# Sending seven attention units of ten, not five, through a DMA transpose, and adding the two output parts on DVE

## The chip, the cores and the metric

One core of one Trainium2 chip runs the kernel. The metric is the device time in microseconds (us) of one execution of the whole program. Names of engines: PE is the matmul engine, DVE the vector engine, ACT the scalar (activation) engine, POOL the GpSimd engine, SP the queue from which most DMAs are issued.

## The reference, cut to what matters

A cross attention with 8 batches, 512 queries, 20 heads of 16 columns, 508 text tokens and 4 image tokens of width 512:

```python
q   = heads(x @ W_q);  k_t = heads(text @ W_k);  v_t = heads(text @ W_v)
probs_t  = softmax(q k_t^T / 4)                       # [8, 20, 512, 508]
text_out = probs_t v_t
qsem = l2norm(probs_t @ text);  sem = qsem @ l2norm(ip)^T
probs_ip = softmax(q k_ip^T / 4 + 0.5 * sem) * spatial_mask
out = (text_out + probs_ip v_ip) @ W_out + b_out + x
```

The norm of `probs_t @ text` is taken without forming it: with the Gram matrix G = text text^T, the squared norm of a query row p is p G p^T.

## The kernel before, in words

**Three stages.** First, for each batch, the projections, G (`u_parts`) and the values (`v_parts`) are made and stored to HBM (until about 345 us). Then comes the main loop, with which the change deals (about 349 to 1686 us). Last, the l2 norms, the image tokens and the output projection (until the end).

**The main loop's unit.** A unit is one head of one batch with 128 query rows: 8 x 20 x 4 = 640 units, in 16 rounds of `ROUND` = 40. In each round the 40 units are written out, and `Fori` loops repeat a round; PE's loops differ from those of the other engines. Each engine has its own hand-written order, and the engines meet in semaphores. For unit j:

- PE, `scores` (L1394): 128x508 scores into one of two banks (`S_BANK`). It waits until `exp` of unit j-2 has read that bank. PE issues it eight units ahead (`LEAD`).
- DVE, `row_maximum` (L1090), then ACT, `exp` (L807), into `probs`, a ring of ten.
- The probabilities are needed turned (tokens on partitions), as the sum of two fp16 parts. There are two ways:
  - **odd j, "turned by DMA"**: ACT copies the high part into `flat` (`flat_hi`, L816), POOL makes the remainder (L579), and SP issues one DMA transpose of both parts (`turn`, L438) into `turned`, a ring of `RING` = 4. For these units ACT adds a constant to the exponent's bias first (`shift`, L796). POOL then adds the remainder onto `probs` as the weight of the norm (`weigh_odd`, L586).
  - **even j, "plain"**: PE turns the fp32 probabilities (`transposes`, L1403, four a unit, three units ahead), ACT takes the high part (`hi`, L832), DVE the remainder (`lo`, L1105); ACT also writes half of the high part of the unturned rows (`halve`, L823), and POOL subtracts it from `probs` (`weigh_even`, L593).
- PE, `unit` (L1428 to L1434): for the high part, four times one matmul with the values into `o` (L1428) and two with G into `y` (L1429, L1430); for the remainder four matmuls with the values (L1434). It waits for the turned data and for the norm of unit j-2 (two `y` banks).
- DVE, `norm` (L1099): `y` times `probs`, summed along the row. DVE's order in step j is `row_maximum(j)`, `norm(j-9)`, and in even steps `lo(j-6)`.
- ACT, `drain_out` (L838): once in two units, the output bank into `out_raw`. POOL, `reduce_head` (L600 a copy of 4 columns, L601 an addition of 128x80), once in four units: the two parts of the output are added into `reduced`.

**Queues.** SP issues the transposes in order, and once in 20 units, after unit 9, ten loads: nine for the next five heads' q and k (`load_group`, L362 and L366) and one for their values (L369). A turn waits for POOL's remainder and for `unit_done` of the unit that last used the slot of the ring.

Of the kernel before, what the change touches and what calls it, by code (L numbers as in the profile page):

```python
# [5 lines left out]
def xattn_kernel(  # L6
# [46 lines left out]
    P = 128  # L53
# [27 lines left out]
    PAIRS_PER_ROUND = ROUND // 2  # L81
# [7 lines left out]
    with stack:  # L89
# [174 lines left out]
        odd_weight_ready = sem("odd_weight_ready")  # L264
        even_weight_ready = sem("even_weight_ready")
# [75 lines left out]

        def nth(rnd, j):

            rnd, j = at(rnd, j)
            return PAIRS_PER_ROUND * rnd + j // 2

        def landed(eng, rnd, j):

            rnd, j = at(rnd, j)
            r = j // 2 % RING  # L350
            need(eng, turned_landed[r], 16 * (PAIRS_PER_ROUND // RING * rnd + j // 2 // RING + 1))

        def flat_rows(j):
            return flat[:, j // 2 % RING]
# [18 lines left out]
        def _(sp):  # L373
# [57 lines left out]
            def turn(rnd, j):  # L431
# [3 lines left out]
                need(sp, unit_done, ROUND * rnd + j + 1 - 2 * RING)  # L435
                apart(sp)
                r = j // 2 % RING
# [57 lines left out]
        def _(pool):  # L495
# [86 lines left out]
            def weigh_odd(rnd, j):  # L582
# [3 lines left out]
                nc.gpsimd.tensor_tensor(own, own, flat_rows(at(rnd, j)[1])[:, 1, :, 0:TP], ALU.add).then_inc(odd_weight_ready, 1)  # L586

            def weigh_even(rnd, j):
# [4 lines left out]
                nc.gpsimd.tensor_tensor(own, own, half_hi[:, at(rnd, j)[1] // 2 % RING, :], ALU.subtract).then_inc(even_weight_ready, 1)  # L593

            def reduce_head(g, slot):

                pool.wait_ge(out_drained, 2 * g + 2)
                apart(pool)
                raw = out_raw[:, 2 * slot:2 * slot + 2].rearrange("p a u c -> p (a u) c")
                nc.gpsimd.tensor_copy(reduced[:, g, :, VW_PART:RCOLS], raw[:, :, VCOLS - 1:VCOLS])  # L600
                nc.gpsimd.tensor_tensor(reduced[:, g, :, 0:VW_PART], raw[:, :, 0:VW_PART],  # L601
                                        raw[:, :, VW_PART:2 * VW_PART], ALU.add).then_inc(head_reduced, 1)

            REDUCE_AT = LEAD + 1 + ST - 1
# [16 lines left out]
            for j in (-6, -4, -2):  # L621
                weigh_even(ROUNDS, j)
# [911 lines left out]
```

## Time and profile before

| what | value |
|---|---|
| median of 3 runs | 1804.03 us (1801.88 to 1806.68) |
| the profiled execution's own time | 1804.91 us |
| its span | 1803.2 us |
| busy: PE / DVE / ACT / POOL | 96% / 69% / 66% / 68% of the span |
| granted clock of PE in the main loop | 0.99 to 1.00 of full speed |

Busy shares are means over the three stages. In the rows below, the third column of a timeline is the engine; `[0.94 <-DVE ...]` behind a row is the idle time of that engine before it and what ended it. Instructions of an engine overlap a little, so the distance between two starts is what an instruction costs its engine, and it is some 0.05 to 0.1 us less than its duration.

### The profile page before, as it was taken

The numbers are of one execution on the slowest core, as the hardware profiler recorded it, in microseconds if no ns is written. First come the engines' busy times: TensorE is split into PE (matmuls) and PEld (weight loads), VectorE is DVE, ScalarE is ACT, GpSimd is POOL, SyncE is SP. The second block draws the span as 40 slices with busy tenths as digits, with TensorE's granted clock in tenths as the row PEclk, the third lists the DMA queues.
The fourth block names the chain that finished last, engine by engine and source line by source line (L and its number), as shares of the span: only waits on it lengthen the run. The fifth ranks groups of instructions, "written<-read, shape, count | busy, mean of one in ns | idle before, by whom it ended". The sixth has DMA issues, their size and how long they took to land.

```text
span 1803.2 us, 48758 instructions
## 1 busy us (share of the span) xinstructions
PE 1736.2 (96%) x14421; PEld 1103.9 (61%) x14421; DVE 1244.6 (69%) x2872; ACT 1182.8 (66%) x2644; POOL 1230.7 (68%) x1414
## 2 busy tenths in 40 slices
PE   4999999599999999999999999999999999999899
PEld 2767666466666666665666666656566666666455
DVE  5445554277777777777777777767677777777684
ACT  2455455477777777777777777777777777777321
POOL 2122212388888888888788888878888888888310
PEclk7999999799999999999999999999999999999999
DMA  5445554734566445445555555465555445553133
GB/s 161 113 139 142 137 144 123 171 68 92 101 103 119 92 91 111 92 91 92 105 92 100 99 121 92 91 106 92 90 90 113 93 91 103 104 96 66 37 103 101
DMA packets 429986, 187.83 MB, mean 104 GB/s; under 512 B 387128, under 2 KB 417472, under 8 KB 429792
## 3 DMA queue, kind: packets, MB, share of 16 engines
q1 hardware_dynamic: 427488, 183.41, 49.4%
q10 hardware_dynamic: 2304, 2.14, 0.4%
q8 instruction: 84, 1.38, 0.3%
q14 instruction: 110, 0.90, 0.2%
HBM read 67.21 MB, written 34.39 MB: 56 GB/s over the span
## 4 chain that ended last, share of the span: by engine, by line
POOL 37%; PE 35%; issue 22%; DVE 3%; POOLq 1%; ACT 1%; DMA 0%; SPq 0%; ACTq 0%; DVEq 0%
POOL probs L586 16%; POOL probs L593 16%; PE bank L1286 13%; PE bank L1429 6%; PE bank L1430 4%; PE bank L1494 3%; POOL reduced L601 2%; POOL wkv L579 2%; PE bank L1344 2%; PE bank L1394 2%; PE bank L1403 1%; PE bank L1495 1%; POOL reduced L600 1%; PE bank L1434 1%; DVE reduced L1017 1%
## 5 line engine op out<-in xcount | busy, mean ns | idle before, releaser
L1429 PE MATMUL bank<-u_sb,late 127*128 127x508 f16 x2560 | 944.0, 375 | 0.0
L1430 PE MATMUL bank<-u_sb,late 127*128 127x508 f16 (+3 forms) x2560 | 761.1, 297 | 0.0
L1090 DVE TENSOR_REDUCE neg_max<-bank 128x1 f32<-128x508 f32 x640 | 439.3, 687 | 342.0 <-PE bank L1394 341.7
L579 POOL TENSOR_TENSOR wkv<-probs,wkv 128x508 f16<-128x508 f32 x320 | 358.8, 1121 | 199.6 <-ACT wkv L816 199.6
L1428 PE MATMUL bank<-v_ring,late 127*128 127x41 f16 x2560 | 468.1, 183 | 4.4 <-DVE late L1105 4.4
L1099 DVE SCALAR_TENSOR_TENSOR probs<-bank,probs 128x508 f32<-128x508 f32 x640 | 432.9, 677 | 4.6 <-PE bank L1430 4.6
L1428 PEld LDWEIGHTS bank<-v_ring,late 127*128 127x128 f16 x2560 | 246.7, 96 | 233.4 <-DVE late L1105 4.5
L593 POOL TENSOR_TENSOR probs<-probs,late 128x508 f32<-128x508 f32 x320 | 368.6, 1152 | 0.0
L586 POOL TENSOR_TENSOR probs<-probs,wkv 128x508 f32<-128x508 f32 x320 | 357.6, 1118 | 0.0
L1429 PEld LDWEIGHTS bank<-u_sb,late 127*128 127x128 f16 x2560 | 247.8, 97 | 166.2 <-issue 1.1
L1394 PE MATMUL bank<-x_sb,work 96*128 96x508 bf16 x640 | 241.8, 378 | 28.2 <-DMA x_sb<-k_parts 12.2
L1430 PEld LDWEIGHTS bank<-u_sb,late 127*128 127x128 f16 x2560 | 244.8, 96 | 0.0
L807 ACT ACTIVATE probs<-bank,neg_max 128x508 f32<-128x508 f32 x320 | 216.8, 677 | 38.7 <-DVE neg_max L1090 20.8
L796 ACT ACTIVATE exp_bias<-neg_max 128x1 f32<-128x1 f32 x320 | 64.7, 202 | 257.1 <-DVE neg_max L1090 257.1
L1105 DVE SCALAR_TENSOR_TENSOR late<-bank,late 127x512 f16<-127x512 f32 x320 | 219.5, 686 | 7.5 <-ACT late L832 7.5
L816 ACT ACTIVATE wkv<-probs 128x508 f16<-128x508 f32 x320 | 201.4, 629 | 25.1 <-ACT probs L807 17.4
L807 ACT ACTIVATE probs<-bank,exp_bias 128x508 f32<-128x508 f32 x320 | 216.2, 676 | 0.0
L1403 PEld LDWEIGHTS bank<-ident,probs 128*127 128x127 f32 x1280 | 190.9, 189 | 9.2
L823 ACT ACTIVATE late<-probs 128x508 f16<-128x508 f32 x320 | 195.8, 612 | 0.7
L1403 PE MATMUL bank<-ident,probs 128*127 128x128 f32 x1280 | 195.1, 275 | 0.0
L546 POOL TENSOR_TENSOR late<-work,late 128x512 bf16<-128x512 f32 (+3 forms) x48 | 55.2, 1151 | 202.9 <-ACT late L723 202.9
L832 ACT ACTIVATE late<-bank 127x512 f16<-127x512 f32 x320 | 184.9, 578 | 0.0
(166 smaller groups left out, 1803.7 us busy)
## 6 DMA issues: line engine op xcount, KB each, us to landing
x_sb<-k_parts SPq DMA_DIRECT2D x192, 79.4 KB, 3.5
x_sb<-in_x SPq DMA_DIRECT2D x16, 640.0 KB, 5.0
reduced<-in_ctx SPq DMA_DIRECT2D x32, 256.0 KB, 5.1
work<-q_parts SPq DMA_DIRECT2D x32, 240.0 KB, 3.4
u_parts<-u_sb SPq DMA_DIRECT2D x8, 825.5 KB, 4.2
u_sb<-u_parts SPq DMA_DIRECT2D x8, 825.5 KB, 5.4
v_parts<-v_sb SPq DMA_DIRECT2D x8, 820.0 KB, 8.0
v_ring<-v_parts SPq DMA_DIRECT2D x32, 205.0 KB, 3.7
```

The costliest lines, as they stand in the source:

```text
L579: nc.gpsimd.tensor_tensor(rows[:, 1, :, 0:TP], probs[:, j % PROB_RING, :].rearrange("p (k t) -> p k t", k=TT), rows[:, 0, :, 0:TP], ALU.su ...
L586: nc.gpsimd.tensor_tensor(own, own, flat_rows(at(rnd, j)[1])[:, 1, :, 0:TP], ALU.add).then_inc(odd_weight_ready, 1)
L593: nc.gpsimd.tensor_tensor(own, own, half_hi[:, at(rnd, j)[1] // 2 % RING, :], ALU.subtract).then_inc(even_weight_ready, 1)
L807: nc.scalar.activation(probs[:, j % PROB_RING, :], bank[S_BANK + j % 2][:, 0:T], ACT.Exp, bias=bias[:, j % 4:j % 4 + 1]).then_inc(probs_re ...
L1090: nc.vector.tensor_reduce(neg_max[:, j % 4:j % 4 + 1], bank[S_BANK + j % 2][:, 0:T], AX.X, ALU.max, negate=True)\
L1099: nc.vector.scalar_tensor_tensor(own, bank[Y_BANK + j % 2][:, 0:T], 1.0 if j % 2 == 1 else 2.0 * PROB_SCALE, own, ALU.mult, ALU.mult, accu ...
L1286: last = nc.tensor.matmul(out, stationary(a), moving(m), start=(n == 1), stop=(n == len(SPLIT) * len(terms)))
L1394: nc.tensor.matmul(bank[S_BANK + j % 2][:, 0:T], q_ring[:, n, h, st * P:(st + 1) * P], k_ring[:, n, h, :], start=True, stop=True).then_inc ...
L1403: last = nc.tensor.transpose(bank[PT_BANK + j // 2 % 2][0:TP, k * P:(k + 1) * P], probs[:, j % PROB_RING, k * TP:(k + 1) * TP], ident[:, :])
L1428: nc.tensor.matmul(o, hi_k, v_ring[0:TP, n, h, k, :], start=(k == 0), stop=False)
L1429: nc.tensor.matmul(y, hi_k, u_sb[0:TP, par, GH[k]:GH[k] + T], start=(k == 0), stop=False)
L1430: done = nc.tensor.matmul(y[:, k * TP:T], hi_k, u_sb[0:TP, par, UL[k]:UL[k] + U_COLS[k]], start=False, stop=(k == TT - 1))
```

## The change

Of each ten units, j mod 10 = 2, 5 and 9 are plain, and the seven others are turned by DMA. All ring indices and counts follow from lists (`OWN[j]` is the number of unit j among those of its kind). The rings keep their sizes, so that a slot of `turned` comes back after four turned units, which are five or six units apart, not eight. POOL's order becomes: remainder of j, weight of a turned unit two steps after it, weight of a plain unit five steps after it. `reduce_head` goes from POOL to DVE, behind `norm` and `lo` in every fourth step. `shift(j+1)` stands ahead of `flat_hi(j)` or `halve(j)` on ACT wherever j+1 is turned. ACT's loop has a last round written out, so that 14 rounds of 16 are in its `Fori` and not 15.

```diff
+    PLAIN_AT = (2, 5, 9)
+    PLAIN = [j for j in range(ROUND) if j % 10 in PLAIN_AT]
+    TURNED = [j for j in range(ROUND) if j % 10 not in PLAIN_AT]
+    OWN = {j: n for kind in (PLAIN, TURNED) for n, j in enumerate(kind)}
...
+        def done_before(rnd, j, back):
+
+            n = OWN[j] - back
+            own = kind(j)
+            return ROUND * (rnd + n // len(own)) + own[n % len(own)] + 1
...
@@ SP: turn, turns
-                need(sp, unit_done, ROUND * rnd + j + 1 - 2 * RING)
+                need(sp, unit_done, done_before(rnd, j, RING))
...
-                for j in range(1, ROUND, 2):
-                    turn(rnd, j)
+                for j in range(ROUND):
+                    if is_turned(j):
+                        turn(rnd, j)
...
@@ POOL
-            def reduce_head(g, slot):
-
-                pool.wait_ge(out_drained, 2 * g + 2)
-                apart(pool)
...
+            TURNED_AT, PLAIN_LAG = 2, 5
 
             def units(rnd, first):
                 for j in range(ROUND):
-                    if j % 2 == 1:
+                    if is_turned(j):
                         remainder(rnd, j)
-                        if not (first and j < 2):
-                            weigh_odd(rnd, j - 2)
-                    elif not (first and j < 6):
-                        weigh_even(rnd, j - 6)
-                    if j % ST == REDUCE_AT % ST and not (first and j < REDUCE_AT):
-                        reduce_head(ROUND // ST * rnd + (j - REDUCE_AT) // ST, (j - REDUCE_AT) // ST % 2)
+                    if is_turned(j - TURNED_AT) and not (first and j < TURNED_AT):
+                        weigh_turned(rnd, j - TURNED_AT)
+                    if not is_turned(j - PLAIN_LAG) and not (first and j < PLAIN_LAG):
+                        weigh_plain(rnd, j - PLAIN_LAG)
...
@@ ACT
-                if not (first and j < 2 * RING):
-                    landed(act, rnd, j - 2 * RING)
-                    need(act, odd_weight_ready, nth(rnd, j) + 1 - RING)
+                if not (first and OWN[j] < RING):
+                    landed(act, rnd, j, 1)
+                    need(act, turned_weight_ready, nth(rnd, j) + 1 - RING)
...
-                need(act, unit_done, ROUND * rnd + j - 3)
-                r = j // 2 % 2
+                need(act, unit_done, done_before(rnd, j, 2))
+                r = OWN[j] % 2
...
                 for j in range(ROUND):
-                    if j % 2 == 1 and not (first and j < HI_AT):
+                    if not is_turned(j - HI_AT) and not (first and j < HI_AT):
                         hi(rnd, j - HI_AT)
+                    if first and j == 0:
+                        shift(rnd, 0)
                     exp(rnd, j)
-                    if j % 2 == 0:
+                    if is_turned(j + 1) and not (last and j + 1 == ROUND):
                         shift(rnd, j + 1)
+                    if is_turned(j):
+                        flat_hi(rnd, j, first)
+                    else:
                         halve(rnd, j)
-                    else:
-                        flat_hi(rnd, j, first)
...
-            units(0, True)
-            with act.Fori(1, ROUNDS) as rnd:
-                units(rnd, False)
...
+            units(0, True, False)
+            with act.Fori(1, ROUNDS - 1) as rnd:
+                units(rnd, False, False)
+            units(ROUNDS - 1, False, True)
...
@@ DVE
+            def reduce_head(g, slot):
+
+                dve.wait_ge(out_drained, 2 * g + 2)
+                apart(dve)
+                raw = out_raw[:, 2 * slot:2 * slot + 2].rearrange("p a u c -> p (a u) c")
+                nc.vector.tensor_copy(reduced[:, g, :, VW_PART:RCOLS], raw[:, :, VCOLS - 1:VCOLS])
+                nc.vector.tensor_tensor(reduced[:, g, :, 0:VW_PART], raw[:, :, 0:VW_PART],
+                                        raw[:, :, VW_PART:2 * VW_PART], ALU.add).then_inc(head_reduced, 1)
+
             LO_AT = 6
+            REDUCE_AT = LEAD + 1 + ST - 1
 
             def units(rnd, first):
                 for j in range(ROUND):
                     row_maximum(rnd, j)
                     if not (first and j < LEAD + 1):
                         norm(rnd, j - LEAD - 1)
-                    if j % 2 == 0 and not (first and j < LO_AT):
+                    if not is_turned(j - LO_AT) and not (first and j < LO_AT):
                         lo(rnd, j - LO_AT)
+                    if j % ST == REDUCE_AT % ST and not (first and j < REDUCE_AT):
+                        reduce_head(ROUND // ST * rnd + (j - REDUCE_AT) // ST, (j - REDUCE_AT) // ST % 2)
...
@@ PE: unit
-                if (j + T_LEAD) % 2 == 0 and not (last and j + T_LEAD >= ROUND):
+                if not is_turned(j + T_LEAD) and not (last and j + T_LEAD >= ROUND):
                     transposes(rnd, j + T_LEAD)
...
-                if j % 2 == 1:
+                if is_turned(j):
                     landed(pe, rnd, j)
```

## Rows read from the trace of the kernel before

**Rows 1.** The page: busy time of each engine over the span.
```profile
PE 1736.2 (96%) x14421; PEld 1103.9 (61%) x14421; DVE 1244.6 (69%) x2872; ACT 1182.8 (66%) x2644; POOL 1230.7 (68%) x1414
```

**Rows 2.** Windows of the main loop: stretch, length, busy (x instructions) by engine, clock, DMA share.
```profile
core 0: us, PE busy (x) PEld busy (x) DVE busy (x) ACT busy (x) POOL busy (x), PEclk, DMA share, GB/s
600.00:800.00 200.00, 199.80 (x1860) 126.67 (x1859) 152.16 (x343) 152.34 (x343) 172.97 (x196) 1.00 0.52 99
```

**Rows 3.** Timeline, PE's scores matmuls and transposes: start, duration.
```profile
1000.99 0.37 PE L1394 MATMUL bank<-x_sb,work 96*128 96x508 bf16 x1
1002.81 0.37 PE L1394 MATMUL bank<-x_sb,work 96*128 96x508 bf16 x1
1003.02 0.60 PE L1403 MATMUL bank<-ident,probs 128*127 128x128 f32 x4
1005.07 0.38 PE L1394 MATMUL bank<-x_sb,work 96*128 96x508 bf16 x1
```

**Rows 4.** PE's idle time in the main loop (350 to 1700 us): total, times, longest.
```profile
PE bank L1394 <- issue: 8.6, 3, 3.3
PE bank L1394 <- ACT probs L807: 6.8, 9, 2.4
```

**Rows 5.** Timeline, POOL, of the same stretch.
```profile
1007.53 1.12 POOL L586 TENSOR_TENSOR probs<-probs,wkv 128x508 f32<-128x508 f32 x1
1008.60 1.15 POOL L593 TENSOR_TENSOR probs<-probs,late 128x508 f32<-128x508 f32 x1
1009.69 0.19 POOL L600 COPY reduced<-out_raw 128x4 f32 x1
1009.84 0.36 POOL L601 TENSOR_TENSOR reduced<-out_raw 128x80 f32 x1
```

**Rows 6.** Timeline, DVE: one even step whole, and the next step's start.
```profile
1001.40 0.69 DVE L1090 TENSOR_REDUCE neg_max<-bank 128x1 f32<-128x508 f32 x1 [0.97 <-PE bank L1394]
1002.00 0.68 DVE L1099 SCALAR_TENSOR_TENSOR probs<-bank,probs 128x508 f32<-128x508 f32 x1
1002.61 0.69 DVE L1105 SCALAR_TENSOR_TENSOR late<-bank,late 127x512 f16<-127x512 f32 x1
1003.22 0.69 DVE L1090 TENSOR_REDUCE neg_max<-bank 128x1 f32<-128x508 f32 x1
```

**Rows 7.** Timeline, ACT, to the end of one loop iteration and the first exp of the next.
```profile
1004.57 0.58 ACT L832 ACTIVATE late<-bank 127x512 f16<-127x512 f32 x1
1005.04 0.68 ACT L807 ACTIVATE probs<-bank,exp_bias 128x508 f32<-128x508 f32 x1
...
1006.28 0.22 ACT L838 ACTIVATE out_raw<-bank 128x82 f32<-128x82 f32 x1
1008.59 0.69 ACT L807 ACTIVATE probs<-bank,neg_max 128x508 f32<-128x508 f32 x1 [2.09 <-DVE neg_max L1090]
```

**Rows 8.** DVE additions and a tensor_scalar of 128x80 after the main loop: ns min/median/max.
```profile
L1165 DVE TENSOR_TENSOR probs<-late,probs x8: 1832/1850/1952, 1690.0 to 1769.2; 128x80 f32<-128x80 f32 x8
L1166 DVE TENSOR_TENSOR probs<-probs x8: 241/242/243, 1691.9 to 1771.1; 128x80 f32<-128x80 f32 x8
L1163 DVE TENSOR_SCALAR probs<-late x8: 193/195/195, 1689.1 to 1768.2; 128x80 f32<-128x80 f32 x4, 128x80 f32 x4
```

**Rows 9.** Timeline after the main loop, POOL and DVE at the same time.
```profile
1689.33 2.42 POOL L638 TENSOR_TENSOR late<-reduced,late 128x1280 f32<-128x1280 f32 x1 [2.60 <-DVE late L1158]
1689.99 1.85 DVE L1165 TENSOR_TENSOR probs<-late,probs 128x80 f32<-128x80 f32 x1
```

**Rows 10.** The transposes' issue on SP (ns min/median/max), and their time to landing.
```profile
L438 SPq DMA_TRANSPOSE late<-wkv x320: 1231/1233/3463, 355.7 to 1669.7; - x160
...
DMA to landing us min/median/max: 3.0/3.0/5.7
```

**Rows 11.** Timeline, SP, around one group's loads.
```profile
1061.19 9.25 SPq L438 DMA_TRANSPOSE late<-wkv  x3
1070.78 1.27 SPq L362 DMA_DIRECT2D work<-q_parts  x3
1077.13 2.83 SPq L438 DMA_TRANSPOSE late<-wkv  x2
```

More of the change, by code:

```diff
@@ L619, in _ @@
                 units(rnd, False)
-            weigh_odd(ROUNDS, -1)
-            for j in (-6, -4, -2):
-                weigh_even(ROUNDS, j)
-            for g in range(HEADS - 1 - (REDUCE_AT - ST) // ST, HEADS):
-                reduce_head(g, g % 2)
+            for j in range(PLAIN_LAG):
+                if j < TURNED_AT and is_turned(j - TURNED_AT):
+                    weigh_turned(ROUNDS, j - TURNED_AT)
+                if not is_turned(j - PLAIN_LAG):
+                    weigh_plain(ROUNDS, j - PLAIN_LAG)
             pool.wait_ge(head_reduced, HEADS)
@@ L821, in halve @@
                 act.wait_ge(probs_ready, ROUND * rnd + j + 1)
[L822 to L823 removed]
+                need(act, plain_weight_ready, nth(rnd, j) + 1 - RING)
+                nc.scalar.activation(half_hi[:, slot_of(j), :], probs[:, j % PROB_RING, :], ACT.Copy, scale=0.5)\
                   .then_inc(half_ready, 1)
@@ L857, in units @@
                         drain_out(ROUND // ST * rnd + g, st // 2, g % 2)
-            units(0, True)
-            with act.Fori(1, ROUNDS) as rnd:
-                units(rnd, False)
-            for u in range(UNITS - DRAIN_AT, UNITS):
-                if u % 2 == 0 and u >= UNITS - HI_AT + 1:
-                    hi(ROUNDS, u - UNITS)
+            units(0, True, False)
+            with act.Fori(1, ROUNDS - 1) as rnd:
+                units(rnd, False, False)
+            units(ROUNDS - 1, False, True)
+            for j in range(DRAIN_AT):
+                if j < HI_AT and not is_turned(j - HI_AT):
+                    hi(ROUNDS, j - HI_AT)
+                u = UNITS + j - DRAIN_AT
                 if u % 2 == 1:
@@ L1122, in _ @@
                 norm(ROUNDS, j - LEAD - 1)
-                if j % 2 == 0 and j < LO_AT:
+                if j < LO_AT and not is_turned(j - LO_AT):
                     lo(ROUNDS, j - LO_AT)
+            for g in range(HEADS - 1 - (REDUCE_AT - ST) // ST, HEADS):
+                reduce_head(g, g % 2)
             dve.wait_ge(head_reduced, HEADS)
@@ L1416, in unit @@
                     pe.wait_ge(values_loaded[n], 16 * (rnd + 1))
-                if j % 2 == 1:
+                if is_turned(j):
                     landed(pe, rnd, j)
-                    both = [turned[0:TP, j // 2 % RING, a] for a in range(2)]
+                    both = [turned[0:TP, slot_of(j), a] for a in range(2)]
                 else:
                     pe.wait_ge(lo_ready, nth(rnd, j) + 1)
-                    both = [a[:, j // 2 % 2, :].rearrange("p (k s) -> p k s", k=TT) for a in (probs_hi, probs_lo)]
+                    both = [a[:, OWN[j] % 2, :].rearrange("p (k s) -> p k s", k=TT) for a in (probs_hi, probs_lo)]
                 need(pe, norms_done, ROUND * rnd + j - 1)
@@ L1444, in _ @@
                 t = j - LEAD + T_LEAD
-                if t >= 0 and t % 2 == 0:
+                if t >= 0 and not is_turned(t):
                     transposes(0, t)
```

50 lines of the change are left out of this document (24 added, 26 removed).

## The prediction

> **What bounds the kernel now.** I read the busy shares first, then the windows, then the timeline. Over the span PE is at 96% and no other engine above 69% [rows 1]. In the main loop the windows say it more sharply: PE 100% busy at full clock, POOL 86%, DVE and ACT 76%, the DMA engines 52% [rows 2]. A busy PE need not be PE at its peak, so the timeline has to show that it doesn't wait: from one scores matmul to the next it takes 1.82 us in a unit without transposes (1000.99 to 1002.81) and 2.26 us in one with them (1002.81 to 1005.07) [rows 3]. So a pair costs 4.08 us, and 320 pairs 1306 us. PE's idle time there that an engine or its own issue caused is only 15 us [rows 4]. PE's instruction stream is the bound, and POOL is the next one.
>
> **1. The transposes that go (gain).** Of ten units three are plain, not five: 640 x 0.2 = 128 units lose their four transposes. One unit's transposes cost PE 2.26 - 1.82 = 0.44 us [rows 3]. 128 x 0.443 = **-56.7 us** (in ten units 19.52 us where it was 20.40). The bound from above is that nothing takes their place; that is what the rest is about.
>
> **2. POOL.** Between starts, a remainder or a weight takes POOL 1.07 us (1007.53 to 1008.60), a plain weight 1.09, and the reduce_head pair about 0.15 + 0.31 = 0.46 [rows 5]. Per ten units before: 10 x 1.07 + 5 x 1.09 + 2.5 x 0.46 = 17.3 of 20.4, 85%, as the window has it [rows 2]. After: 14 x 1.07 + 3 x 1.09 = 18.25 of 19.52, 93.5%. With reduce_head kept it would be 19.4, no room at all. POOL keeps up, with 1.3 us spare in ten units. I went through its order by hand: at most two jobs pile up (remainder 0, weight 8, plain weight 5 in a row), which makes remainder 1 about 1.3 us late, and that is gone by unit 3. Nobody needs a remainder that soon (see 5). Cost 0; if the cover goes, rival C.
>
> **3. ACT and DVE.** ACT per ten units by durations: it loses two hi and two halve and gets two flat_hi and two shifts, 88% full before and after; in between I find every exp done about 1 us ahead of the scores matmul that waits for it. Cost 0. What does change is the place where ACT's loop turns. Today the first exp of an iteration starts 2.09 us after the last instruction of the one before (drain 1006.28 + 0.22, exp 1008.59) [rows 7], and PE hardly feels it: PE's waits for exp are 6.8 us in nine places [rows 4]. The cover is thin: this exp starts 3.5 us after its scores (1005.07) and the scores matmul that needs it comes 4.08 us after them. After the change the iteration ends on shift(0) of the next round, which can't run before row_maximum of that unit, 1.10 us after its scores (0.41 to the start, 0.69 long) [rows 3, 6]; halve and drain follow, then the 2.1 us, then hi(35) takes 0.47 us of ACT before exp (1004.57 to 1005.04) [rows 7]. By that exp ends some 5.2 us after its scores, where PE wants it after 4.08: 1.15 us of stall at each of 13 turns, 15 us, less some 4 that it costs already: **+11 us**. Bounds: 0 (the turn stays hidden, as now) and 13 x 1.7 = 22, if DVE's own turn makes the row maximum late by 0.5 as well. The Trainium skill, "Runtime: NRT & Kernel Launch", section "Instruction fetch mechanics", says that a taken branch out of the prefetched window stalls the sequencer; by that, too, the stall is at the turn alone, and the 2.09 us agree.
>
> **4. reduce_head on DVE.** The trace has no such pair on DVE in the loop. Its cost in DVE's own time is small: an addition of 128x80 takes 0.24 us [rows 8], a tiny copy some 0.1 more. But the same rows have another addition of the same shape, L1165, that takes 1.85 us all eight times. The timeline shows why: it starts 0.66 us after a POOL instruction of 2.42 us (1689.33 to 1691.75) and ends at 1691.84, 0.09 after it [rows 9]. Both its inputs lie in SBUF, as those of reduce_head's addition do; norm and lo have one input in PSUM and run at 0.68 beside a POOL that is 86% busy [rows 2, 6]. So I take it that reduce_head's addition waits until the POOL instruction under way ends, and POOL is now under way 93% of the time. The Trainium skill ("SBUF — State Buffer", on who interferes with whom) states it as a lock: a DVE instruction with two SBUF inputs and a GpSimd instruction that reads SBUF exclude each other. The rows agree.
>
> What does it cost the path? DVE's step after a scores matmul at time 0: row_maximum at 0.41, norm at 1.01, done at 1.7 (lo, where there is one, at 1.62) [rows 3, 6]. PE must not start a unit's y matmuls before norm of two units earlier; with units of 1.82 us that norm has about 0.3 us of slack, 0.75 where the unit is 2.26 long. A reduce_head in a step delays the next row_maximum and with it the next norm. Going through the five reduce steps of 20 units with POOL's order from part 2: in step 8, which has lo ahead of it, the addition waits for remainder 7, the next step is 0.85 us late, and PE stalls 0.55; in the four others the lateness is 0 to 0.4, mostly within the slack, together 0.1. That is 0.65 us in 20 units, x 32 = **+21 us**. Lower bound 0 (no meeting, as with L1166), upper bound for this one wait: a whole POOL instruction, 1.07 less 0.3 slack, for each of 160 heads, 123 us. I take 21 because a wait has a mean of half an instruction and four of five steps can swallow that.
>
> **5. The transposes that come.** 448 in place of 320. SP's issue takes 1.23 us each [rows 10], 7 x 1.23 = 8.6 of 19.5 us: fits. The data moves in a small part of the 3.0 us to landing; the DMA share of 52% [rows 2] goes to some 70%. The slot of `turned` is now released by a unit that is five or six ahead, not eight: the turn starts at the latest four units before its own (7.3 to 7.7 us) and lands after 3.0 [rows 10]. Covered, but for unit 10 after the loads: turn 8 waits for unit 3; issue 1.23, then the ten loads, 6.7 us from the end of one turn (1061.19 + 9.25) to the start of the next (1077.13) [rows 11], then 3.0 to 5.7 to landing [rows 10]. That is 11.2 to 13.9 us after the start of unit 4, and PE wants it after 12.0. Up to 1.9 us late in each of 31 places, mostly not at all: **+3 us** (0 to 59).
>
> **Sum.** 1804.9 (the profiled execution's time; 1.7 above its span, 0.9 above the median) - 56.7 + 11 + 21 + 3 = 1783; less the 0.9 it is **1782** against the median.
>
> **The rivals.**
> A. *The lock costs nothing that counts* (DVE's addition falls into POOL's gaps). Then the sum lacks 21: 1761. For it: 24% of DVE's loop is idle [rows 2]. Against: L1165, eight of eight [rows 8].
> B. *Slower: DVE waits twice for each head.* The copy ahead of the addition is an SBUF to SBUF instruction, too. If it also waits for POOL's instruction, POOL's next one is queued by then and goes ahead of the addition, which waits a whole 1.07 us more. Its place is the step after each reduce; hardly any slack is left there, so nearly all of it reaches PE: 160 x (1.07 less about 0.1) = 155 on top of the forecast, 1937; less where POOL has gaps by then, from 1850. It decides from 0.26 us of PE stall a head on: (56.7 - 11 - 3)/160 is where the gain is used up. For it: a tensor_scalar of 128x80 between SBUF and SBUF takes 195 ns, the addition 242 [rows 8], so one-input instructions run in another, faster way. Against: no row has such a copy beside POOL. The Trainium skill, same page and section, says that a copy between SBUF and SBUF in a two-port mode excludes GpSimd wholly; by that rule this rival is what happens, if four elements are enough for the mode, which no row here shows.
> C. *POOL becomes the bound*: 18.25 us, its own turn of the loop (some 2 us in 40 units, 0.5 in ten), and what DVE's additions block, 2.5 x 0.3. That makes 19.5, level with PE; each 0.5 us of ill-timed idle in ten units is 32 us: about 1795.
> D. *Late landings after the loads*: the upper end of part 5, +56: about 1838, slower. For it: landings of 5.7 occur. Against: the median is 3.0.
>
> **How the numbers follow.** A measurement of this kernel can tell 0.3% (5.4 us) from no change. Chances: the forecast 0.45, A 0.20, B 0.18, C 0.11, D 0.06. The range goes from 1755 (A with a hidden loop turn) to 1838 (D and the dearer ends of parts 3 and 4) and leaves out B. Faster than 1798.6: most of the forecast (0.41), all of A, 0.08 of C: 0.69. Within 0.3%: 0.07. Slower: B, D: 0.24.
>
> **What would show it.** Right: PE at 1.82 and 2.26 us a unit, with 768 transposes and not 1280; POOL at 91 to 94% in the windows; DVE's 128x80 addition far over 0.24 us in the mean (0.6 to 0.8) and PE stalls behind norm, once in 20 units and at ACT's turn. Wrong: the copy of 4 columns at 0.5 us or more and the addition over 1.1 (B), POOL without gaps (C), PE idle until a DMA landing (D), or the addition at 0.24 (A). That the two kinds are not 7 to 3 can't be: the lists fix it.

## The result, and the profile after the change

The changed kernel takes 1870.03 us (median of 4 runs, 1865.09 to 1873.23), where the kernel before takes 1804.12 on the same chip: a ratio of 1.0368 [1.0339, 1.0397]. It is 66 us slower. The forecast was 1782, within 1755 to 1838, so sign and range were both wrong. The profiled execution took 1873.23, its span is 1871.5.

The page of the changed kernel: busy time of each engine, to be held against [rows 1], and from its costliest groups the copy of `reduce_head` (busy us, mean ns | idle before it, and what ended most of it):

```profile
span 1871.5 us, 48870 instructions
PE 1711.9 (91%) x13909; PEld 1045.4 (56%) x13909; DVE 1335.6 (71%) x3064; ACT 1140.2 (61%) x2644; POOL 1291.7 (69%) x1222
...
L1127 DVE COPY reduced<-out_raw 128x4 f32 (+1 forms) x160 | 119.1, 745 | 53.1 <-ACT out_raw L846 51.9
```

The windows of the main loop, same columns as [rows 2]:

```profile
core 0: us, PE busy (x) PEld busy (x) DVE busy (x) ACT busy (x) POOL busy (x), PEclk, DMA share, GB/s
600.00:800.00 200.00, 183.55 (x1640) 109.37 (x1641) 151.54 (x343) 135.27 (x319) 167.19 (x153) 0.97 0.65 112
```

PE has 512 records fewer (128 units times four transposes), as planned. But in the loop it is now busy 92% of the time and not 100%, and POOL, which was to rise to 93.5%, is at 84%: nobody is full any more. An engine that was the bound and has become idle says that a wait was added. The next view names it. PE's waits from 350 to 1760 us, that is, in the main loop (engine, line, what it waited for: us in total, times, longest):

```profile
PE bank L1456 <- DVE probs L1113: 52.3, 76, 2.4
PE bank L1422 <- ACT probs L815: 29.1, 19, 2.7
PE bank L1456 <- issue: 14.5, 17, 1.4
PE bank L1456 <- DMA late<-wkv: 9.1, 10, 1.4
```

Where [rows 4] had 6.8 and 8.6 us, there is now a unit's first matmul (L1456) waiting for norm (L1113), the scores matmul (L1422) waiting for exp (L815), and a little for landings. Idle time counts from the end of the last record; the distance between starts shows the whole of a stall. So I took, for every unit, the distance from its scores matmul to its first own matmul less the shortest that occurs (0.21 us, or 0.65 with transposes between them), and the distance from the end of the unit before to the scores matmul:

| PE's stalls in the loop, us | before | after |
|---|---|---|
| first matmul of a unit waits for norm | 3.8 (no single one over 0.2) | 91.2 (132 times, those with a late landing among them) |
| scores matmul waits for exp, at the turn of ACT's loop | 2.8 | 24.3 |
| late landing of a transpose | 0 | 10.4 |
| other, at the loop's start | 8.9 | 6.4 |
| stretches in which PE runs at 1.2 GHz (granted clock 0.50) | 3.4 long | 30.6 long |

The stalls grew by 116.8. At 1.2 GHz PE's matmuls take up to twice as long (from a scores matmul to the unit's first own 0.40 us at 779.38, where it is 0.21 at full clock). PE is busy for 27.4 of these 30.6 us, and for 3.0 of the 3.4 before; half of the difference, about 12, is what the clock costs, by estimate. With the gain: -56.7 + 116.8 + 12 = +72, and the loop, from its first unit to its last, grew by 66.6 (1324.4 to 1391.0). The sum is 5 too high; that a part of the slow stretches is counted in the stalls as well would explain it, but isn't shown.

**The wait for norm.** Of the 91.2 us, 22.5 lie in unit 33 of each round, at the loop turn. The rest sits in four units of twenty, those whose number mod 20 is 10 (23.9, the late landings included), 14 (22.2), 18 (21.6) and 2 (7.9). A `reduce_head` in step j makes norm(j-8) late, for which PE waits ahead of unit j-6: these are steps 16, 0, 4 and 8. The fifth, step 12, costs nothing. The timeline of the changed kernel shows one whole (start, duration, engine):

```profile
1005.71 0.22 ACT L846 ACTIVATE out_raw<-bank 128x82 f32<-128x82 f32 x1
1005.88 1.12 POOL L598 TENSOR_TENSOR wkv<-probs,wkv 128x508 f16<-128x508 f32 x1
1006.16 0.38 PE L1422 MATMUL bank<-x_sb,work 96*128 96x508 bf16 x1
1006.19 0.83 DVE L1127 COPY reduced<-out_raw 128x4 f32 x1 [0.60 <-ACT out_raw L846]
1006.94 0.23 DVE L1128 TENSOR_TENSOR reduced<-out_raw 128x80 f32 x1
1006.96 1.19 POOL L605 TENSOR_TENSOR probs<-probs,wkv 128x508 f32<-128x508 f32 x1
1007.09 0.67 DVE L1104 TENSOR_REDUCE neg_max<-bank 128x1 f32<-128x508 f32 x1
1007.68 0.67 DVE L1113 SCALAR_TENSOR_TENSOR probs<-bank,probs 128x508 f32<-128x508 f32 x1
1007.97 0.37 PE L1422 MATMUL bank<-x_sb,work 96*128 96x508 bf16 x1
1008.61 0.19 PE L1456 MATMUL bank<-v_ring,late 127*128 127x41 f16 x1 [0.26 <-DVE probs L1113]
```

The copy of four columns starts at 1006.19 and ends at 1007.02, 0.02 after POOL's instruction (1005.88 + 1.12). The addition slips into the gap and takes its 0.23. The row maximum starts 0.93 us after its scores matmul (1006.16 to 1007.09) instead of 0.41, so 0.52 late; norm is as late; and PE's first matmul comes 0.64 after its scores instead of 0.21, 0.43 late. Without the wait the pair would have ended at about 1006.6, just when row_maximum is due. All 160 of them (ns min/median/max), from two views of the changed kernel:

```profile
L1127 DVE COPY reduced<-out_raw x160: 166/836/1149, 368.7 to 1751.2; 128x4 f32 x150, 128x4 f32<-128x4 f32 x10
L1128 DVE TENSOR_TENSOR reduced<-out_raw x160: 226/229/1234, 369.3 to 1751.3; 128x80 f32 x150, 128x80 f32<-128x80 f32 x10
```

The copy takes 0.17 us free and 0.745 in the mean, by the page's last row above; the addition 0.428 in the mean (68.5 us over 160) at a median of 0.229: it is mostly free, and in some heads waits for a second instruction. The pair's waits add up to (745 - 166 + 428 - 229) x 160 = 124 us. The same row's idle time is the other half: 51.9 us in which DVE sits idle for ACT's drain before the copy can start.

**The loop turn.** Timeline of the changed kernel around 950 us, DVE, ACT and PE's scores matmuls. Unit 0 of a round has its scores at 950.63:

```profile
949.82 0.68 DVE L1113 SCALAR_TENSOR_TENSOR probs<-bank,probs 128x508 f32<-128x508 f32 x1
950.63 0.38 PE L1422 MATMUL bank<-x_sb,work 96*128 96x508 bf16 x1
952.89 0.37 PE L1422 MATMUL bank<-x_sb,work 96*128 96x508 bf16 x1
952.98 0.69 DVE L1104 TENSOR_REDUCE neg_max<-bank 128x1 f32<-128x508 f32 x1 [2.47 <-issue]
953.70 0.20 ACT L804 ACTIVATE exp_bias<-neg_max 128x1 f32<-128x1 f32 x1 [2.37 <-DVE neg_max L1104]
954.33 0.22 ACT L846 ACTIVATE out_raw<-bank 128x82 f32<-128x82 f32 x1
956.78 0.60 ACT L840 ACTIVATE late<-bank 127x512 f16<-127x512 f32 x1 [2.23 <-PE bank L1462]
957.27 0.68 ACT L815 ACTIVATE probs<-bank,exp_bias 128x508 f32<-128x508 f32 x1
958.00 0.39 PE L1422 MATMUL bank<-x_sb,work 96*128 96x508 bf16 x1 [1.83 <-ACT probs L815]
959.91 0.37 PE L1422 MATMUL bank<-x_sb,work 96*128 96x508 bf16 x1
```

Two turns stand one behind the other. DVE goes back to the start of its loop: idle 2.47 us with "issue" behind it, and the row maximum starts 2.35 us after its scores. ACT's shift of the same unit waits for it (2.37), then halve and drain run, and only then does ACT turn, 2.23 us more. (The label names PE; but the `hi` behind the gap needs transposes that were done before. What ended this gap is ACT's own return.) Exp starts 6.64 us after its scores. The scores matmuls of units 1 and 2 are 5.11 us apart, where 1.82 is normal. At the 13 turns of ACT's loop the distance is 4.88 to 6.43 us, 3.5 more than normal in the mean, some 46 us in all. These are the two entries of the table: PE waits for norm of unit 31, which stands on DVE behind the late row maximum (the 22.5 us of unit 33), and then for ACT's exp (24.3).

Why DVE's turn has become long can be seen, too. The page calls the packets of queue 14 "instruction": they load code. Here are their numbers (packets, MB, share of 16 engines' span) in the kernel before, in the changed one and in the one with the pair left out, an experiment below; then the row maximum at a turn in that last kernel, which is not late:

```profile
q14 instruction: 110, 0.90, 0.2%
q14 instruction: 184, 1.51, 0.3%
q14 instruction: 113, 0.93, 0.2%
...
916.44 0.69 DVE L1104 TENSOR_REDUCE neg_max<-bank 128x1 f32<-128x508 f32 x1 [0.62 <-PE bank L1423]
```

By the trace's DMA records, in the changed kernel one packet of queue 14 starts in DVE's gap at each of its 14 turns, 0.4 to 0.6 us after DVE's last instruction (1.2 at one turn). It takes 0.31 us in most and up to 1.47, and the row maximum starts 1.7 to 1.8 us after the packet's end. The whole gap is 2.4 to 3.7 us. In the kernel before and in the one without the pair no packet falls into DVE's gap at any turn, and the gap is 1.06 and 0.62 us. So DVE's turn wasn't merely hidden there, it was short. ACT's turn has such a packet at every turn in both kernels, and is as long before as after (2.0 to 2.5 us).

A PE that idled can run slowly afterwards, as it does behind 5 of the 14 turns here (behind the one shown above it doesn't). The windows around another turn of the changed kernel (stretch, busy time of PE, weight load, DVE, ACT, POOL, then the granted clock):

```profile
769.00:773.00 4.00, 4.00 (x39) 2.57 (x38) 1.29 (x3) 2.36 (x5) 4.00 (x4) 1.00 1.30 115
773.00:777.00 4.00, 1.58 (x16) 0.75 (x12) 2.16 (x6) 0.84 (x3) 2.40 (x3) 0.99 0.35 75
777.00:783.00 6.00, 4.47 (x26) 2.26 (x25) 2.72 (x7) 3.79 (x8) 2.78 (x3) 0.50 0.23 45
```

PE is busy 1.58 us of four, and in the next stretch the granted clock is 0.50: the scores matmul there takes 0.61 us and not 0.37.

The landings, ns in the first line, us in the last, against [rows 10]:

```profile
L456 SPq DMA_TRANSPOSE late<-wkv x448: 1231/1232/3278, 352.4 to 1739.6; - x150
...
DMA to landing us min/median/max: 3.0/3.1/6.8
```

### The profile page after: what moved, and what is told of

Read it like the earlier page. It is cut to its first block, busy times and chain, and to the rows that moved or that the text cites. A ratio compares the mean times of both kernels' runs of the same rounds, so it can differ in the third digit from the quotient of the medians.

```text
span 1871.5 us, 48870 instructions
## 1 busy us (share of the span) xinstructions
PE 1711.9 (91%) x13909; PEld 1045.4 (56%) x13909; DVE 1335.6 (71%) x3064; ACT 1140.2 (61%) x2644; POOL 1291.7 (69%) x1222
## 3 DMA queue, kind: packets, MB, share of 16 engines
q1 hardware_dynamic: 562656, 216.98, 59.5%
## 4 chain that ended last, share of the span: by engine, by line
POOL 41%; PE 31%; issue 22%; DVE 3%; ACT 1%; POOLq 1%; DMA 1%; SPq 1%; DVEq 0%; ACTq 0%
POOL wkv L598 17%; POOL probs L605 16%; PE bank L1314 12%; POOL probs L612 7%; PE bank L1457 5%; PE bank L1522 3%; PE bank L1458 3%; PE bank L1372 2%; PE bank L1523 1%; PE bank L1422 1%; PE bank L1431 1%; PE bank L1456 1%; DVE reduced L1031 1%; PE bank L1462 1%; PE bank L1507 0%
## 5 line engine op out<-in xcount | busy, mean ns | idle before, releaser
L598 POOL TENSOR_TENSOR wkv<-probs,wkv 128x508 f16<-128x508 f32 x448 | 500.8, 1118 | 207.6 <-ACT wkv L824 206.1
L1456 PE MATMUL bank<-v_ring,late 127*128 127x41 f16 x2560 | 470.0, 184 | 76.8 <-DVE probs L1113 52.3
L605 POOL TENSOR_TENSOR probs<-probs,wkv 128x508 f32<-128x508 f32 x448 | 497.9, 1117 | 0.0
L1456 PEld LDWEIGHTS bank<-v_ring,late 127*128 127x128 f16 x2560 | 247.3, 97 | 343.7 <-issue 113.7
L1113 DVE SCALAR_TENSOR_TENSOR probs<-bank,probs 128x508 f32<-128x508 f32 x640 | 431.7, 675 | 7.4 <-PE bank L1458 7.4
L815 ACT ACTIVATE probs<-bank,exp_bias 128x508 f32<-128x508 f32 x448 | 302.3, 675 | 0.0
L824 ACT ACTIVATE wkv<-probs 128x508 f16<-128x508 f32 x448 | 279.3, 624 | 26.4 <-DMA late<-wkv 9.8
L1422 PE MATMUL bank<-x_sb,work 96*128 96x508 bf16 x640 | 243.5, 381 | 47.2 <-ACT probs L815 29.1
L612 POOL TENSOR_TENSOR probs<-probs,late 128x508 f32<-128x508 f32 x192 | 225.3, 1174 | 1.3 <-PE bank L1431 1.3
L1462 PEld LDWEIGHTS bank<-v_ring,late 127*128 127x128 f16 x2560 | 131.0, 96 | 76.8 <-issue 2.4
L1462 PE MATMUL bank<-v_ring,late 127*128 127x41 f16 x2560 | 166.3, 182 | 0.0
L1127 DVE COPY reduced<-out_raw 128x4 f32 (+1 forms) x160 | 119.1, 745 | 53.1 <-ACT out_raw L846 51.9
L815 ACT ACTIVATE probs<-bank,neg_max 128x508 f32<-128x508 f32 x192 | 129.6, 675 | 36.1 <-DVE neg_max L1104 34.4
L1119 DVE SCALAR_TENSOR_TENSOR late<-bank,late 127x512 f16<-127x512 f32 x192 | 131.4, 684 | 17.5 <-ACT late L840 17.4
L840 ACT ACTIVATE late<-bank 127x512 f16<-127x512 f32 x192 | 112.3, 585 | 29.1 <-PE bank L1462 28.8
```

Source lines behind the costliest of these rows:

```text
L598: nc.gpsimd.tensor_tensor(rows[:, 1, :, 0:TP], probs[:, j % PROB_RING, :].rearrange("p (k t) -> p k t", k=TT), rows[:, 0, :, 0:TP], ALU.su ...
L605: nc.gpsimd.tensor_tensor(own, own, flat_rows(j)[:, 1, :, 0:TP], ALU.add).then_inc(turned_weight_ready, 1)
L612: nc.gpsimd.tensor_tensor(own, own, half_hi[:, slot_of(j), :], ALU.subtract).then_inc(plain_weight_ready, 1)
L815: nc.scalar.activation(probs[:, j % PROB_RING, :], bank[S_BANK + j % 2][:, 0:T], ACT.Exp, bias=bias[:, j % 4:j % 4 + 1]).then_inc(probs_re ...
L824: nc.scalar.activation(flat_rows(j)[:, 0, :, 0:TP], probs[:, j % PROB_RING, :].rearrange("p (k t) -> p k t", k=TT), ACT.Copy).then_inc(fla ...
L1113: nc.vector.scalar_tensor_tensor(own, bank[Y_BANK + j % 2][:, 0:T], 1.0 if is_turned(j) else 2.0 * PROB_SCALE, own, ALU.mult, ALU.mult, ac ...
```

## The experiments

**Theory 1** puts the larger part of the loss on the pair's wait for POOL's instruction, with the loop turn on top. Its rivals are that seven of ten are too many in themselves (POOL too full, landings), so that it would be slow without the pair as well; and that the addition alone waits (the forecast's form) and not the copy. Ratios are against the kernel before on the same chip, from three rounds each; that kernel takes 1801.7 to 1805.1 on the four chips, so that times from two chips compare to some 3 us.

**The pair left out.** DVE only signals; the wait for the drain stays. The addition of the two parts is left out, and `reduced` is filled with ones after the loop.

```diff
-nc.vector.tensor_copy(reduced[:, g, :, VW_PART:RCOLS], ...)
-nc.vector.tensor_tensor(reduced[:, g, :, 0:VW_PART], ...).then_inc(head_reduced, 1)
+dve.sem_inc(head_reduced, 1)
```

> Left out: the adding of the output's two parts and the copy of the row sums (DVE only waits for ACT's drain and counts up; after the loop it fills the sums' tile with ones, 128x13440, some 14 us outside the loop by the rate of DVE's other instructions). Theory 1 (DVE's copy waits for POOL's instruction under way, right ahead of the thin slack of norm, and that makes most of PE's new idle time): the 75 us of waits for norm at units 2, 10, 14 and 18 of 20 go, the loop's turns stay at least in part: 1870 - 75 - up to 20 + 14 = 1790 to 1810, PE idle at its wait for norm under 30 us. Theory 2 (the seven turned units of ten themselves slow the loop, by the smaller lead of the transposes and a full POOL): 1850 to 1885.

1795.36 us, ratio 0.9948 [0.9921, 0.9975]. The fill is not free, as its row in the timeline says:

```profile
1663.98 11.26 DVE L1152 MEMSET reduced<- 128x13440 f32 x1 [3.02 <-issue]
```

Less these 14.3 us it is 1781. The stalls for norm fell from 91.2 to 4.2, and the loop is 93 us shorter than the changed kernel's. So the pair's instructions cause the loss, not the seven in ten and not the wait for the drain alone. But this run takes away two things at once: POOL's hold on the pair, and DVE's long turn. PE's waits of this kernel (400 to 1650 us) have only the turn and the landings left:

```profile
PE bank L1423 <- ACT probs L815: 22.9, 13, 2.7
PE bank L1457 <- DMA late<-wkv: 6.7, 5, 2.1
```

Here DVE's row maximum at the turn starts 0.50 us after its scores, as before the change: DVE's turn is short, and ACT's alone is left. The scores matmuls at the turn are 3.44 to 4.71 us apart, 1.9 more than normal in the mean.

**The pair on DVE in the kernel before** (five of ten, same steps).

```diff
@@ kernel before
-reduce_head on POOL
+reduce_head on DVE, behind norm and lo, in every fourth step
```

> The kernel before with one part of the change alone: the two parts are added on DVE, in the same steps; five of ten stay plain. Theory 1: half of the units have transposes ahead of the wait for norm, so the slack is 0.6 to 0.75 us in every second unit and POOL is under way less; DVE's copy still waits, mean 0.4 to 0.8 us where it costs 0.17 alone: 1820 to 1850. Theory 2: 1804, within 6.

1817.48 us, 1.0082 [1.0053, 1.011]: slower, by less than expected. The copy, ns min/median/max:

```profile
L1098 DVE COPY reduced<-out_raw x160: 161/316/951, 364.9 to 1692.6; 128x4 f32 x150, 128x4 f32<-128x4 f32 x10
```

The median is 0.32 here and 0.84 in the changed kernel, so in mid-round the pair hardly waits. The stalls for norm are 16.2 us, 11.7 of them in units 33 and 34, at the turn: with the pair in its loop, DVE loads code at each of its turns here as well (180 packets of queue 14 where there were 110), and the row maximum comes 1.4 to 1.7 us after its scores and not 0.50. So most of the 13 us are DVE's turn and not the wait for POOL, which the expectation had as the cause.

**The copy as a reduction over one element**, the addition as it is: only the addition has two SBUF inputs now.

```diff
-nc.vector.tensor_copy(reduced[:, g, :, VW_PART:RCOLS], raw[:, :, VCOLS - 1:VCOLS])
+nc.vector.tensor_reduce(reduced[:, g, :, VW_PART:RCOLS], raw[:, :, VCOLS - 1:VCOLS], AX.X, ALU.add)
```

> The changed kernel; the copy of four columns is a tensor_reduce over one element, the 128x80 addition stays a tensor_tensor with both inputs in SBUF. Theory 1a (both kinds wait for POOL, whichever comes first takes the wait): the addition now has 0.6 us more in the mean, 0.8 us, the time is that of the changed kernel within 1%: 1855 to 1880. Theory 1b (only the copy's two-port form waits in the loop; the addition had 0.23 us there): the addition stays at 0.23 and the time falls to 1775 to 1800.

1836.07 us, 1.0175 [1.0127, 1.0224]: a miss for the time expected, 34 us under the changed kernel. The rows:

```profile
L1127 DVE TENSOR_REDUCE reduced<-out_raw x160: 153/161/166, 368.1 to 1717.7; 128x4 f32 x150, 128x4 f32<-128x4 f32 x10
L1128 DVE TENSOR_TENSOR reduced<-out_raw x160: 233/774/1192, 368.1 to 1717.8; 128x80 f32 x150, 128x80 f32<-128x80 f32 x10
```

The wait has moved: the first instruction never waits, the second takes 0.698 in the mean. The pair takes 0.86 us, not 1.17, because it can meet only one POOL instruction; the stalls for norm fall to 59.5. So both forms wait, each for whatever POOL has under way, and the copy in front costs a second wait in some heads.

**Both as reductions.** The addition becomes a sum over two elements of one input.

```diff
-nc.vector.tensor_tensor(reduced[:, g, :, 0:VW_PART], raw[:, :, 0:VW_PART], raw[:, :, VW_PART:2 * VW_PART], ALU.add)
+nc.vector.tensor_reduce(reduced[:, g, :, 0:VW_PART],
+                        raw[:, :, 0:2 * VW_PART].rearrange("p s (a c) -> p s c a", a=2), AX.X, ALU.add)
```

> The changed kernel; copy and addition are both tensor_reduce instructions with one SBUF input (over one and over two elements). The same results, no POOL contention if it hangs on a second SBUF port. Theory 1: 0.15 and 0.25 to 0.3 us each, the waits for norm at units 2, 10, 14 and 18 of 20 fall from 75 us to under 20, the time is 1775 to 1805, and this beats both kernels. Theory 2: 1850 to 1880, the mean durations fall but the time doesn't follow.

1801.31 us, 0.9983 [0.9956, 1.001]: 69 us back. The second row:

```profile
L1128 DVE TENSOR_REDUCE reduced<-out_raw x160: 311/325/330, 367.3 to 1679.9; 128x160 f32 x150, 128x80 f32<-128x160 f32 x10
```

It is 0.1 us longer than a free addition and never waits: 160 times between 0.311 and 0.330, beside a POOL that is 90% busy. The kernel's stalls are 28.8 us for norm, 21.9 of them in unit 33, and 21.6 for exp at the turn: what is left is the turn, beside 6.0 us of late landings. It doesn't beat the kernel before, as was expected of it.

**The rounds written out**, DVE's and ACT's, so that neither turns; alone, and with the reductions. The round's number is then a constant, and so is the column that norm writes (`norms[:, v:v + 1]`).

```diff
-with act.Fori(1, ROUNDS - 1) as rnd:
+for rnd in range(1, ROUNDS - 1):
...
-with dve.Fori(1, ROUNDS) as rnd:
+for rnd in range(1, ROUNDS):
```

> The changed kernel with DVE's and ACT's rounds written out, so that neither engine's loop turns; nothing else. Theory 1 (at each turn DVE's row maximum comes 2.4 us after its scores and not 0.4, and ACT's turn stands behind it, together 3.3 us of PE time at each of 13 turns, some 43 us): 1815 to 1835, and the long step behind scores of unit 1 of a round is gone. Theory 2 (that time is DVE's waiting for POOL, seen at the turn by chance): 1855 to 1875.

> As b1, with the copy and the addition as tensor_reduce (a4). Theory 1: a4's 1801 less the same 43: 1750 to 1770, near the sum without any wait (1748 = 1804.9 - 56.7), and faster than both kernels. Theory 2: 1790 to 1801.

Alone: 1834.06 us, 1.0176 [1.013, 1.0223]; stalls for exp at the turn 0 and in unit 33 0.1, the others for norm 91, where the changed kernel has 69 outside unit 33. With the reductions: **1747.93 us, 0.971 [0.9656, 0.9764]**, 54 us faster than the kernel before on the same chip and 122 faster than the changed one. Its windows and its copy, now a reduction:

```profile
600.00:800.00 200.00, 198.60 (x1854) 122.26 (x1853) 156.35 (x389) 150.69 (x357) 187.74 (x173) 1.00 0.71 128
```

PE is full again, at full clock, with POOL at 94% and the DMA engines at 71%, as parts 2 and 5 of the prediction had it. PE's waits of this kernel (350 to 1640 us):

```profile
PE bank L1423 <- issue: 6.1, 2, 3.1
PE bank L1457 <- DMA late<-wkv: 4.7, 8, 1.4
PE bank L1423 <- ACT probs L815: 4.5, 5, 1.8
```

The four kernels of this square give both effects twice. The wait costs 69 us with the turns there (1870.0 to 1801.3) and 86 without (1834.1 to 1747.9); the turns cost 36 with the wait there and 53 without it. That either way sums to 122 follows from the four times. What the square shows is that the two effects alone, 69 and 36, are less than the 122 of both: stalls of the one kind cover some of the other.

**Norm ahead of row_maximum**, since norm seemed to be what PE waits for.

```diff
-row_maximum(rnd, j)
 norm(rnd, j - LEAD - 1)
+row_maximum(rnd, j)
```

> The changed kernel with DVE's order norm(j-9), then row_maximum(j). If what makes DVE's wait for POOL so dear is that norm has only 0.3 us of slack behind the row maximum, norm now has some 1 us, and the 75 us of waits for norm fall to under 30, the exp pays at most its own slack: 1800 to 1835. If exp has no slack either, the stall moves to the scores matmuls: 1860 to 1900.

1910.28 us, 1.0594 [1.0547, 1.064]: a clear miss. DVE's waits (420 to 1750 us) say why:

```profile
DVE reduced L1127 <- ACT out_raw L846: 145.8, 147, 1.2
DVE probs L1113 <- PE bank L1458: 102.0, 120, 3.0
```

Norm first makes DVE wait for PE's `y`, and for the drain in nearly every head, with the row maximum queued behind both. The stalls for exp are then 78 us and those for norm 75.7. Exp has no slack to give away either.

**The pair back on POOL**, with seven of ten.

```diff
-reduce_head on DVE
+reduce_head on POOL, in the same steps
```

> Seven of ten turned, the two parts added on POOL as before. POOL has 19.4 us of work in 19.5. Theory 1 (DVE waits and DVE's dearer turn come with the pair on DVE): PE's waits for norm are few, POOL 97% busy or more in the windows and the loop runs at POOL's pace, 19.6 to 20.2 us in ten units, plus ACT's turn of 1.6 us: 1780 to 1815. Rival (a full POOL drags everything, the move was needed): 1830 to 1870.

1827.26 us, 1.0131 [1.0085, 1.0177], between the two expectations. POOL is 92% busy (183.20 of 200), and 56.4 of 60.8 us of stalls for norm are in unit 33. There a new wait shows, of norm for POOL's weight, from DVE's waits:

```profile
DVE probs L1127 <- POOL probs L605: 26.3, 11, 2.9
```

In mid-round POOL keeps up. That it has no room to catch up in after the turns would explain the rest, but no run separates that. DVE loads code at its turns here, too (183 packets of queue 14). With seven of ten the pair's place is thus worth 1827 us on POOL, 1870 on DVE as it was moved, and 1801 on DVE with the wait gone: what cost the time is the form in which it was moved, not that it was.

**Which turn, and whether it matters before.** DVE's rounds alone written out, ACT's alone, both in the kernel before, and POOL's in addition to the fastest version; each the edit above for the engines named.

> The changed kernel with DVE's rounds written out, ACT's loop kept. b1, with both written out, gained 36 us. Theory 1 (DVE's turn is the new part: its row maximum comes 2 us late, and ACT's turn stands behind it): DVE's share is some 20 to 25 us, 1845 to 1852; PE still stalls some 1.6 us at ACT's turn. Theory 2 (all of it is ACT's turn, DVE's is covered): 1865 to 1873.

> The changed kernel with ACT's rounds written out, DVE's loop kept. Theory 1 (the two turns add up): 1840 to 1855, norm of unit 31 of a round still late. Theory 2 (ACT's turn is all): 1830 to 1838, as b1. Theory 3 (either turn alone is as dear as both): 1862 to 1873.

> The kernel before (five of ten, the parts added on POOL) with DVE's and ACT's rounds written out. PE waited only some 3 us for the turns there, so 1798 to 1804; then b2's 1748 is the doing of seven in ten, not of the rounds written out. Rival: the turns cost more than PE's waits show, 1780 or less.

> b2 (both tensor_reduce, DVE's and ACT's rounds written out) with POOL's rounds written out as well. POOL has 1.3 us of room in ten units and its turn is some 1 us in 40: if that is covered, 1745 to 1751, the same; if POOL's lateness behind its turn reaches PE, 1735 to 1744.

| kernel | us | ratio | row maximum after its scores, at the turn |
|---|---|---|---|
| changed, DVE written out | 1840.38 | 1.0202 [1.0161, 1.0242] | 0.41 |
| changed, ACT written out | 1855.33 | 1.0281 [1.0243, 1.0319] | 2.4 |
| before, both written out | 1801.73 | 0.9992 [0.9969, 1.0015] | |
| fastest, POOL written out too | 1750.63 | 0.9715 [0.967, 0.9761] | |

Against 1870.0, DVE's turn is worth 30 us, ACT's 15, both 36; the first two fell outside what was expected, by 5 and by 0.3. Each edit removes its own stall whole: with DVE written out that of unit 33 is gone and that for exp stays (the scores at the turn are 3.44 to 4.76 us apart, as in the kernel without the pair), with ACT written out it is the other way round. Removing ACT's gains less because the stalls elsewhere grow: the first matmuls outside unit 33 wait 77 us in the changed kernel (landings included), 71 with DVE written out, 93 with ACT and 94 with both. In the kernel before, the same edit gains nothing that can be told from zero, so the 54 us of the fastest version are the doing of the seven in ten. POOL's turn is covered even where POOL is 94% busy.

## Why the prediction was wrong, point by point

**Part 1, the transposes (-56.7): right.** The fastest version takes 1747.9, and 1804.9 - 56.7 is 1748.2. That it fits to 0.3 us is luck (its runs span 1741 to 1755), but the main loops say the same: 1324.4 us before and 1267.8 there, 56.6 less. The gain is there in the changed kernel too, and is outweighed. One reading was short: [rows 4] leave out a third entry of that view, 4.4 us in two places in which PE waits for `lo`, so that the idle time was 20 us and not 15; nothing hangs on it.

**Part 2, POOL (0): right.** POOL takes 94% in the fastest version and PE doesn't feel it; rival C did not happen.

**Part 4, `reduce_head` on DVE (+21): this is the step that failed.** The mechanism was right in kind: DVE's instruction waits until POOL's ends. The size was 69 to 86 us, still under the upper bound of 123. Three sentences of it fell:
- "I take it that reduce_head's *addition* waits": the copy of four columns waits just as well, and being first it takes most of the wait (0.58 us in the mean, the addition 0.20). This is rival B's place. The forecast noted that the copy is an SBUF to SBUF instruction and gave B 0.18, for want of a row with a copy beside POOL. But B's double wait, an addition of 0.9 us or more, happens in 32 of the 160 heads, and its 1850 to 1937 came from a whole instruction more in every one. Its range holds the result; its price per head doesn't. The Trainium skill ("SBUF — State Buffer", "Who interferes with whom") has the addition's wait, and says of a copy that it can take the two-port mode and wait as well; that this mode is what made the copy of four columns wait, no run shows. It has the remedy, too: that page says that `tensor_reduce` never contends on trn2, and 320 of them here did not.
- "A wait has a mean of half an instruction and four of five steps can swallow that": the mean fits (0.58 against 1.07/2), but one can't walk through the steps with means. The engines run locked to each other; in step 16 the copy takes 1.10 to 1.14 us in 30 of 32 rows. And the pair can't start when DVE is free: it waits for ACT's drain, 50.4 us in 92 places, up to 0.6 each. The wait for POOL begins only after that. The slack before norm absorbs the drain by itself: with both as reductions, the stalls for norm outside unit 33 are 7 us. With the drain it has little left, and of the 124 us of waits that come on top, some 69 reach PE. Four of the five steps stall; step 8, which the forecast took for the one dear step, is the cheapest of the four.
- The forecast's walk through the steps let each pair start when DVE was done with its step. The drain's place on ACT's timeline ([rows 7] shows one) was never set against the end of norm, though the pair has to wait for both.

DVE's wait for the drain, in the changed kernel (350 to 1700 us), beside its long waits for scores:

```profile
DVE neg_max L1104 <- PE bank L1422: 210.2, 292, 4.3
DVE reduced L1127 <- ACT out_raw L846: 50.4, 92, 0.6
DVE neg_max L1104 <- issue: 25.1, 10, 2.6
```

The first row is the trap of the 24% idle that spoke for rival A: DVE idles 210 us for scores and still makes PE wait, since its idle time lies before the scores and the pair behind them.

**Part 3, the loop turn (+11, 0 to 22): right in place, too small.** ACT's turn by itself costs 1.9 us each in the kernel without the pair, 25 in all: over the upper bound, not the 1.15 taken. What was missing is DVE's own turn. The bound allowed the row maximum 0.5 us of lateness, after the trace of before, where no code is loaded at that turn and the row maximum comes 0.50 us after its scores. In the changed kernel it comes 2.3 to 3.6 us after them (the last row above, 25.1 us in 10 places). PE then stalls twice, for norm of unit 31 (22.5 us in all) and for exp (24.3). The two turns together cost 36 us by the runs, 53 with the wait for POOL gone. The Trainium skill ("Runtime: NRT & Kernel Launch", "Instruction fetch mechanics") says that a taken branch out of the prefetched window has to wait for a fetch of its target, and that this is one reason why kernels prefer full unrolling. The trace agrees on the fetch: a code packet in each gap of the long turns of DVE, and none in those of the short ones. Unrolling pays here only once PE leaves no slack: in the kernel before, the edit gave 0.9992. Why DVE's loop loads code at its turn with the pair on POOL and doesn't without the pair, though the loop with the pair on POOL holds no more work, stays open.

**Part 5, landings (+3, 0 to 59): near enough.** 10.4 us in the changed kernel, about 5 in the fastest. One reading in it was wrong: the data of a transpose doesn't move in a small part of the 3.0 us. In the kernel before, the packets of one run from about 1.2 to 2.5 us after the start of its issue, with all 16 DMA engines busy.

**Not in the sum at all: the clock.** 30.6 us at 1.2 GHz, where there were 3.4, cost some 12 us by the estimate above.

**The sum.** 1804.9 - 56.7 = 1748, where the fastest version is, and the wait and the turns bring the 122 from there to 1870 by the four runs, clock and landings with them. The forecast had 32 for the two. What it said would show B ("the copy of 4 columns at 0.5 us or more and the addition over 1.1") came true by half: 0.745 and 0.428. PE at 1.82 and 2.26 us a unit held wherever nothing waited.

## What to carry to other kernels

Beside a busy POOL, write small SBUF work on DVE with one input and as a reduction: here a two-input addition, or even a copy of four columns, cost up to a whole POOL instruction on top of its own time. Before work is moved into an in-order queue, look at the slack of the instruction that will stand behind it, at the moment when its input arrives, and not at the engine's idle share. When a change takes slack out of a pipeline or puts instructions into a loop, price every engine's loop turn anew: count the code packets on the page, and follow each instruction behind the turn to the one that waits for it.

## What the runs showed of the hardware that was not expected

- A copy of 128x4 fp32 between SBUF and SBUF takes 0.17 us free and up to 1.15 beside POOL; as a reduction over one element 0.15 to 0.17, always.
- The turn of a loop of 40 units has two lengths on DVE. In the changed kernel a code packet falls into the gap at each of 14 turns, and the gap is 2.4 to 3.7 us; without the pair there is no packet and the gap is 0.62 us. ACT's is 2.0 to 2.5 us in the changed kernel, with a packet each time. With the rounds written out, PE stalls at none of these places.
- PE, having idled, goes on at 1.2 GHz in some places (the granted clock is 0.50 for 3.4 or 6.8 us): behind 5 of 14 turns in the changed kernel, behind 14 of 14 with the pair on POOL, where PE's gaps at the turn are longest. In all it is 30.6 us in the changed kernel, 58 with norm first, 75 with the pair on POOL and 6.8 in the fastest.
